# Zero-tile matmuls at the start, projection weights in quarters and a ring of six PSUM banks in a linear-attention and routed-FFN layer

## What is computed

```python
xn = _layernorm(x, axis=-1)
q = _phi((x @ W_Q.T).reshape(b, t, H, DK))      # attention: x is xn here
k = _phi((x @ W_K.T).reshape(b, t, H, DK))
v = (x @ W_V.T).reshape(b, t, H, DK)
S = g4 * S + jnp.einsum('bhi,bhj->bhij', kt, vt)     # scan over tokens
z = g3 * z + kt
num = jnp.einsum('bhij,bhi->bhj', S, qt)
den = jnp.sum(z * qt, axis=-1, keepdims=True) + EPS
y = (num/den * sigmoid(x @ W_g_w.T + W_g_b)) @ W_O.T
# FFN on xn: base = x @ W_lin.T + b_lin; top 2 of 8 experts, each left (D x 4), right (4 x D)
x = x + attention(xn) + ffn(xn)
```

## Time and profile before

| | us |
|---|---|
| median of 3 runs | 265.98 (265.62 to 266.72) |
| the profiled execution | 264.92 |
| its span, slowest core (core 3) | 263.9 |
| spans of the 8 cores | 262.6 to 263.9 |
| TensorE busy | 243.6 (92%) |
| VectorE / ScalarE / GpSimd busy | 162.8 / 79.5 / 61.7 |

### The profile page before, as it was taken

One profiled execution on the slowest core, in us unless ns is written; L12 is line 12 of the kernel. 1 busy time (PEld: TensorE's weight loads), 2 busy tenths in 40 slices (PEclk: granted clock), 3 DMA queues, 4 the chain that ended last, 5 costly groups with the idle time before them and its releaser, 6 DMA issues.

```text
span 263.9 us, 5412 instructions; the slowest of 8 cores (262.6 to 263.9 us)
## 1 busy us (share of the span) xinstructions
PE 243.6 (92%) x1768; PEld 122.6 (46%) x1768; DVE 162.8 (62%) x425; ACT 79.5 (30%) x132; POOL 61.7 (23%) x99
## 2 busy tenths in 40 slices
PE   0369999999889999999999999999999999999995
PEld 0233444454444555454545454445545555544442
DVE  5646374858766667565664657546556685686622
ACT  2644857375445222324333022111111201000000
POOL 2773000030505501314050403021304030333000
DMA  6999999999994022120404022122222123343223
GB/s 183 238 142 253 243 166 226 208 194 178 254 345 149 0 83 79 70 92 0 161 1 157 4 82 79 79 83 81 79 82 82 80 80 106 137 137 105 82 97 142
DMA packets 9615, 33.25 MB, mean 126 GB/s; under 512 B 1458, under 2 KB 1778, under 8 KB 9332
## 3 DMA queue, kind: packets, MB, share of 16 engines
q1 hardware_dynamic: 6692, 22.27, 24.8%
q0 software_dynamic: 2896, 10.64, 21.4%
HBM read 32.00 MB, written 8.39 MB: 153 GB/s over the span
## 4 chain that ended last, share of the span: by engine, by line
PE 84%; DVE 7%; issue 3%; DMA 3%; ACT 1%; SPq 0%; DVEq 0%; ACTq 0%
PE PJ L340 26%; PE L L362 17%; PE L L406 8%; PE PJ L333 7%; PE PJ L362 4%; PE L L340 4%; DMA x_sb<-x 3%; PE T L311 3%; PE L L333 2%; PE SY L354 2%; PE PJ L406 2%; PE T L347 2%; PE SY L378 1%; PE T L319 1%; PE T L392 1%
## 5 line engine op out<-in xcount | busy, mean ns | idle before, releaser
L362 PE MATMUL L<-wlin_sb,xnfm 128*128 128x512 bf16 x208 | 49.2, 379 | 0.0
L298 POOL TENSOR_SCALAR S_blk<-S_sb,small_s 128x260 bf16<-128x260 f32 x30 | 28.8, 973 | 85.8 <-DVE S_sb L775 85.6
L362 PEld LDWEIGHTS L<-wlin_sb,xnfm 128*128 128x128 bf16 x208 | 19.8, 98 | 23.2 <-issue 0.8
L844 ACT ACTIVATE e_sb<-PJ 128x512 bf16<-128x512 f32 x28 | 16.5, 593 | 42.1 <-PE PJ L340 40.6
L608 DVE TENSOR_SCALAR e_sb<-e_sb 128x512 bf16<-128x512 bf16 x32 | 9.4, 294 | 28.7 <-ACT e_sb L844 28.7
L820 ACT ACTIVATE xn_tm<-x_sb,nmr,rstd 128x1024 bf16<-128x1024 f32 x16 | 19.9, 1241 | 23.6 <-POOL nmr L254 22.1
L406 PE MATMUL L<-wo_sb,ygfm 128*128 128x512 bf16 x104 | 26.7, 379 | 0.0
L340 PE MATMUL PJ<-xnfm,wg_sb 128*128 128x512 bf16 x112 | 26.6, 379 | 0.0
L340 PE MATMUL PJ<-xnfm,wq_sb 128*128 128x512 bf16 x112 | 26.6, 380 | 0.0
L340 PE MATMUL PJ<-xnfm,wk_sb 128*128 128x512 bf16 x112 | 26.6, 380 | 0.0
L333 PE MATMUL PJ<-wv_sb,xnfm 128*128 128x512 bf16 x96 | 24.6, 400 | 0.0
(11 more groups left out here) (115 smaller groups left out, 357.0 us busy)
## 6 DMA issues: line engine op xcount, KB each, us to landing
ro_sb<-x SPq DMA_DIRECT2D x16, 512.0 KB, 4.0
out<-ro_sb SPq DMA_DIRECT2D x15, 512.0 KB, 2.7
x_sb<-x SPq DMA_DIRECT2D x10, 512.0 KB, 8.8
x_sb<-x POOLq DMA_DIRECT2D x6, 512.0 KB, 21.3
wlin_sb<-wlin POOLq DMA_DIRECT2D x1, 2048.0 KB, 38.9
wv_sb<-wv POOLq DMA_DIRECT2D x4, 256.0 KB, 10.9
wq_sb<-wq POOLq DMA_DIRECT2D x2, 512.0 KB, 18.2
wk_sb<-wk POOLq DMA_DIRECT2D x2, 512.0 KB, 24.7
```

The lines of the kernel that those rows point to most:

```text
L298: GP.tensor_scalar(S_blk[:, :].rearrange("p (q w) -> p q w", q=4)[:, :, 65 * e : 65 * e + 65], S_sb[:, :].rearrange("p (q w) -> p q w", q= ...
L362: TE.matmul(lb(c, n)[:, :], xnk(k, c), wlin_sb[:, D * k + 512 * n : D * k + 512 * n + 512], start=False, stop=False)
L844: SE.activation(e_sb[:, 512 * (n % 2) : 512 * (n % 2) + 512], bank[:, :], AF.Exp).then_inc(ac_e, 1)
```

## The change

Zero-tile matmuls (`warm`) run ahead of the first transpositions and at two later places; every projection weight comes in quarters, GpSimd's queue interleaves x4 to x7 with them and first waits for x1; SP's `small`, `cmat` and blin wait for the second quarter of wq. rstd of chunks 1 and 3 is made by GpSimd between its transfers. Six banks rotate. The programs of TensorE, VectorE and ScalarE for the opening are put in another order. The diff, cut to its core:

```diff
-    ring4 = [PJ[0], PJ[1], L[0], L[1]]
+    ring6 = [PJ[0], PJ[1], L[0], L[1], SYb[0], SYb[1]]
+    vb = [ring6[i] for i in (0, 1, 2, 3, 2, 1, 2, 1)]
+    qb = [ring6[i] for i in (4, 5, 0, 1)]
+    kb = [ring6[i] for i in (3, 4, 5, 0)]
+    gb = kb
...
         load_x(3)
+        SY.wait_ge(d_wq[1], 16)
         SY.dma_start(small[:, :], small_d[:, :]).then_inc(d_sm, 16)
...
-        SY.wait_ge(d_wg[1], 16)
+        SY.wait_ge(d_wg[3], 16)
...
+    def wload_q(dst, srcd, i, s):
+        o = 2 * FH * i
+        GP.dma_start(dst[:, o : o + 2 * FH], srcd[:, o : o + 2 * FH]).then_inc(s[i], 16)
...
     def rs(c):
+        j = {1: 0, 3: 1}.get(c, c - 6)
         GP.wait_ge(dv_st, c + 1)
...
-        GP.wait_ge(d_x[0], 16)
...
+        GP.wait_ge(d_x[1], 16)
+        wload_q(wv_sb, wv_d, 0, d_wv)
+        wload_q(wv_sb, wv_d, 1, d_wv)
+        rs(1)
+        wload_q(wv_sb, wv_d, 2, d_wv)
+        wload_q(wv_sb, wv_d, 3, d_wv)
+        wload_q(wq_sb, wq_d, 0, d_wq)
+        wload_q(wq_sb, wq_d, 1, d_wq)
+        rs(3)
         xload(4)
+        wload_q(wq_sb, wq_d, 2, d_wq)
+        wload_q(wq_sb, wq_d, 3, d_wq)
+        wload_q(wk_sb, wk_d, 0, d_wk)
+        wload_q(wk_sb, wk_d, 1, d_wk)
         xload(5)
-        wload_half(wq_sb, wq_d, 1, d_wq)
+        wload_q(wk_sb, wk_d, 2, d_wk)
+        wload_q(wk_sb, wk_d, 3, d_wk)
         xload(6)
+        wload_q(wg_sb, wg_d, 0, d_wg)
+        wload_q(wg_sb, wg_d, 1, d_wg)
         xload(7)
...
+    def warm(n):
+        for _ in range(n):
+            TE.matmul(SYb[1][:, :], S_blk[:, 0:128], S_blk[:, 0:512], start=True, stop=True)
...
     def pe_program():
+        TE.wait_ge(dv_z, 1)
+        warm(22)
         TE.wait_ge(d_id, 16)
         xtr(0)
+        warm(5)
         xtr(1)
...
+        TE.wait_ge(d_wv[0], 16)
+        vproj(0, vb[0], 0, 2)
+        warm(2)
+        TE.wait_ge(d_wv[1], 16)
+        vproj(0, vb[0], 2, 4)
...
+        TE.wait_ge(d_wv[3], 16)
+        for c in range(3):
+            vproj(c, vb[c], 6, 8)
+        TE.wait_ge(dv_xev, 4)
+        vproj(3, vb[3])
+        for i in range(4):
+            TE.wait_ge(d_wq[i], 16)
+            for m in range(4):
+                if i == 0 and m >= 2:
+                    TE.wait_ge(ac_v, m - 1)
+                fproj(wq_sb, 0, m, qb[m], pe_q, 2 * i, 2 * i + 2)
         xtr(4)
+        TE.wait_ge(ac_v, 4)
+        for i in range(4):
+            if i == 2:
+                TE.wait_ge(dv_xev, 5)
+                vproj(4, vb[4])
+            TE.wait_ge(d_wk[i], 16)
+            for m in range(4):
+                if i == 0 and m >= 1:
+                    TE.wait_ge(dv_q, m)
+                fproj(wk_sb, 0, m, kb[m], pe_k, 2 * i, 2 * i + 2)
+            if i == 2:
+                xtr(5)
         TE.wait_ge(dv_xev, 6)
+        TE.wait_ge(dv_q, 4)
+        vproj(5, vb[5])
+        for i in range(4):
+            TE.wait_ge(d_wg[i], 16)
+            for m in range(4):
+                if i == 0:
+                    TE.wait_ge(dv_k, m + 1)
+                fproj(wg_sb, 0, m, gb[m], pe_g, 2 * i, 2 * i + 2)
+            if i == 0:
+                xtr(6)
+            if i == 1:
+                TE.wait_ge(dv_xev, 7)
+                TE.wait_ge(ac_v, 5)
+                vproj(6, vb[6])
+            if i == 2:
+                xtr(7)
         TE.wait_ge(d_lg, 16)
         tgp(0)
-        for c in (6, 7):
-            TE.wait_ge(dv_xev, c + 1)
-            TE.wait_ge(ac_g, c - 5)
-            vproj(c, L[c - 6])
+        TE.wait_ge(dv_xev, 8)
+        TE.wait_ge(ac_v, 6)
+        vproj(7, vb[7])
...
     def dve_program():
+        VE.memset(S_blk[:, :], 0.0).then_inc(dv_z, 1)
...
         xev_v(3)
+        stats(4)
         VE.wait_ge(d_sm, 16)
...
+        phi(0, qb[0], fm(qfm, 0)[:, 0:512], dv_q)
+        phi(1, qb[1], fm(qfm, 0)[:, 512:1024], dv_q)
         VE.wait_ge(ac_dec, 2)
         VE.tensor_scalar(dk8a[:, :], nlg[:, 0:8], small[:, 16:17], None,
                          ALU.mult).then_inc(dv_dec, 1)
+        xev_v(4)
+        phi(2, qb[2], fm(qfm, 0)[:, 1024:1536], dv_q)
+        phi(3, qb[3], fm(qfm, 0)[:, 1536:2048], dv_q)
         VE.wait_ge(d_cm, 16)
...
         ins.then_inc(dv_mk, 1)
-        stats(4)
         stats(5)
...
         xev_v(5)
...
         stats(6)
+        for m in range(4):
+            phi(4 + m, kb[m], fm(kfm, 0)[:, 512 * m : 512 * m + 512], dv_k)
+        xev_v(6)
         stats(7)
-        VE.wait_ge(ac_mk, 1)
+        VE.wait_ge(ac_dec, 3)
         qt(0)
...
         for c in range(4):
             xn(c)
+        for c in range(4):
+            vev(c, vb[c])
+        SE.wait_ge(d_sm, 16)
+        SE.activation(nlg[:, :], small[:, 4:16], AF.Exp, scale=-1.0).then_inc(ac_dec, 1)
+        xn(4)
...
+        for m in range(2):
+            SE.wait_ge(pe_q, m + 1)
+            eexp(m, qb[m])
         SE.wait_ge(dv_dec, 2)
         SE.activation(dk8[:, :], dk8a[:, :], AF.Exp)
         SE.activation(gc4[:, :], nlg[:, 8:12], AF.Exp, scale=-128.0)
+        for m in range(2, 4):
+            SE.wait_ge(pe_q, m + 1)
+            eexp(m, qb[m])
         SE.wait_ge(d_cm, 16)
...
         SE.activation(masks[:, :], mtmp, AF.Exp).then_inc(ac_mk, 1)
...
         xn(5)
+        vev(4, vb[4])
         for m in range(4):
+            if m == 2:
+                xn(6)
+            SE.wait_ge(pe_k, m + 1)
+            eexp(4 + m, kb[m])
+        vev(5, vb[5])
         xn(7)
+        vev(6, vb[6])
         for m in range(4):
-            tanhg(0, m, ring4[(m + 2) % 4])
+            tanhg(0, m, gb[m])
         xn(8)
+        vev(7, vb[7])
         e8exp(0)
```

More of the change, by code:

```diff
@@ L131, in build_core @@
     d_lg = sem("d_lg")
-    d_wv, d_wq, d_wk, d_wg = ([sem(f"d_wv{i}") for i in range(4)], [sem("d_wqa"), sem("d_wqb")],
-                              [sem("d_wka"), sem("d_wkb")], [sem("d_wga"), sem("d_wgb")])
+    d_wv, d_wq = [sem(f"d_wv{i}") for i in range(4)], [sem(f"d_wq{i}") for i in range(4)]
+    d_wk, d_wg = [sem(f"d_wk{i}") for i in range(4)], [sem(f"d_wg{i}") for i in range(4)]
+    dv_z = sem("dv_z")
     d_wl, d_wo, d_rt = sem("d_wl"), sem("d_wo"), sem("d_rt")
@@ L412, in kproj @@
     def kproj(c):
-        TE.wait_ge(ac_g, c + 4)
+        if c == 0:
+            TE.wait_ge(ac_v, 8)
+        else:
+            TE.wait_ge(ac_g, c + 4)
         fproj(wk_sb, c // 4 + 1, c % 4, PJ[1], pe_k)
@@ L464, in pe_program @@
[L464 to L467, removed]
-        TE.wait_ge(dv_xev, 3)
-        xtr(4)
[L470 to L489, removed]
-        TE.wait_ge(dv_xev, 6)
[L491 to L499, removed]
+        TE.wait_ge(d_wv[0], 16)
[3 more added lines that the diff above has]
+        vproj(0, vb[0], 2, 4)
+        TE.wait_ge(dv_xev, 2)
+        vproj(1, vb[1], 0, 4)
+        xtr(2)
+        TE.wait_ge(d_wv[2], 16)
+        for c in range(2):
+            vproj(c, vb[c], 4, 6)
+        TE.wait_ge(dv_xev, 3)
@@ new lines, in pe_program @@
+        vproj(2, vb[2], 0, 2)
+        xtr(3)
+        vproj(2, vb[2], 2, 6)
+        TE.wait_ge(d_wv[3], 16)
[9 more added lines that the diff above has]
+                fproj(wq_sb, 0, m, qb[m], pe_q, 2 * i, 2 * i + 2)
+        xtr(4)
+        TE.wait_ge(ac_v, 4)
@@ L517, in pe_program @@
                 TE.wait_ge(dv_norm, c)
+            else:
+                TE.wait_ge(ac_g, 3)
             scores(c)
@@ L595, in stats @@
         VE.wait_ge(dv_st, c + 1)
-        if c < 8:
+        if c < 8 and c not in (1, 3):
             VE.tensor_scalar(nm[:, c : c + 1], mv[:, 2 * c : 2 * c + 1], -1.0, None,
@@ L704, in dve_program @@
         ins.then_inc(dv_mk, 1)
-        stats(4)
         stats(5)
-        xev_v(4)
-        for m in range(2):
-            phi(m, ring4[m], fm(qfm, 0)[:, 512 * m : 512 * m + 512], dv_q)
         xev_v(5)
-        for m in range(2, 4):
-            phi(m, ring4[m], fm(qfm, 0)[:, 512 * m : 512 * m + 512], dv_q)
         stats(6)
+        for m in range(4):
+            phi(4 + m, kb[m], fm(kfm, 0)[:, 512 * m : 512 * m + 512], dv_k)
+        xev_v(6)
         stats(7)
-        VE.wait_ge(ac_mk, 1)
+        VE.wait_ge(ac_dec, 3)
         qt(0)
-        for m in range(4):
-            phi(4 + m, ring4[(m + 2) % 4], fm(kfm, 0)[:, 512 * m : 512 * m + 512], dv_k)
-        xev_v(6)
         xev_v(7)
@@ L802, in xn @@
     def xn(c):
-        if c < 8:
+        if c < 8 and c not in (1, 3):
+            j = {0: 0, 2: 1}.get(c, c - 2)
             SE.wait_ge(dv_st, c + 1)
@@ L871, in act_program @@
             xn(c)
+        for c in range(4):
[3 more added lines that the diff above has]
+        xn(4)
         SE.wait_ge(dv_ini, 4)
-        SE.activation(nlg[:, :], small[:, 4:16], AF.Exp, scale=-1.0).then_inc(ac_dec, 1)
         SE.wait_ge(dv_dec, 1)
         SE.activation(nlg[:, :], nlg[:, :], AF.Ln, bias=one_c[:, :]).then_inc(ac_dec, 1)
+        for m in range(2):
+            SE.wait_ge(pe_q, m + 1)
+            eexp(m, qb[m])
         SE.wait_ge(dv_dec, 2)
```

58 lines of the change are left out of this document (13 added, 45 removed).

## The result

The changed kernel takes 277.92 us (median; 277.83 to 278.32), the kernel before, on the same chip, 265.92: a ratio of 1.0449, 95% interval 1.0424 to 1.0474. The forecast of 270.7 us had the direction; its range ended at 274.0. The profiled execution took 277.9 us, its slowest core (0) spans 276.7.

What follows compares the result with a forecast made beforehand. TensorE bounds the end, VectorE `tgp` to iteration 1. E 29.7, plus 29.2 to `tgp` and 15.6 to iteration 1, loses 4.75 us: 264.92 becomes 269.7, plus 1.06 to the median, 270.7 us; range 266.5 to 274.0.

Steps and rivals of the forecast that it cites:

- E: Start of the first exponential of q on ScalarE; forecast at 29.7 us, against 33.23 before.
- `small` at 22.3 + 0.1 + 4.0: On SP's queue, `small` waits for wq's second quarter (22.3), then takes 4.0 us like a residual row, landing at 26.4.
- a rival (0.07): On SP's queue `small` takes 8.6 us to land: +9.35 us, 275.3 us in all; chance 0.07.
- its sum 1.2 us lower: If DMA engines take queues in turn, `small` lands in about one turn and the sum is 1.2 us lower.
- The clock: TensorE's clock falls in waits of k's and g's first quarters; the one behind g costs 1.9 us: 272.6 us; chance 0.17.
- The chain from E to `tgp`: Evacuations make TensorE wait for banks and xn(5) in k and g: `tgp` starts at E + 29.2, against 20.9 before.
- Zero for the zero tiles: Opening: ten slow matmuls may speed up, worth 1.9 us of TensorE, but nothing on the path, since q awaits its weights.
- Zero for one v less behind `tgp`: Behind `tgp` `vproj(7)` stands alone where two did; costs nothing, since VectorE is the limit there.
- 27.5: Earliest E by DMA order: wq's last quarter lands at 26.9, then 2 matmuls; would give +2.6 us.
- 28.5: E if x4 decides: x4 lands at 23.9, then statistics 1.6, normalization 2.57 and Ln 0.4 us.
- v would end near 23.5 as before: If zero tiles do not raise the clock: v ends near 23.5, q's first block at 29.1, still before 29.7.
- break-even of 24.95: Value of E at which iteration 1, at E + 44.8, starts at 69.75 us as before.

Runs made afterwards that it cites:

- experiment 5: Changed kernel with `small` issued early and the decay tables and masks put back ahead of q on ScalarE and VectorE: 272.67 us, ratio 1.0234.
- experiments 3 and 4: 3: changed kernel without its 29 zero-tile matmuls, 278.52 us, ratio 1.0458. 4: kernel before with 22 and 5 zero-tile matmuls alone, 266.26 us, ratio 0.9992.
- experiment 1: Changed kernel without SP's wait for wq's second quarter, so small, cmat and blin are issued behind x3 again: 275.05 us, ratio 1.0336.
- experiment 11: Changed kernel, `small` early, tables ahead of q, phi of k first, v(6) behind `tgp`, x10 and x11 on GpSimd's queue ahead of wlin: 267.80 us, ratio 1.0075.

## Why the prediction was wrong in size

The steps of the prediction against core 0 of the changed kernel (a `*` marks core 2, where the clock held behind g's first quarter):

| step | forecast | measured |
|---|---|---|
| SP issues `small` | 22.4 us | 23.55 |
| `small` lands | 26.4 | 33.3 |
| E | 29.7 | 36.03 |
| k's first quarter ends | E + 5.6 | E + 5.56 |
| xtr(5) ends | E + 13.1 | E + 13.2 |
| g's first quarter ends | E + 21.4 | E + 21.8 (21.5*) |
| `tgp` starts | E + 29.2 | E + 30.8 (29.3*) |
| `tgp` to iteration 1 | 15.6 | 15.85 |
| iteration 1 to the third | 11.3 | 11.29 |

- **The step that failed** is the term "`small` at 22.3 + 0.1 + 4.0". wq's second quarter came 1.2 us later than its sum of bytes gave; then `small` took 9.7 us to land, 7.7 to 9.7 on the eight cores, where I had taken 4.0 from a residual row because that was alone in its queue. The same transfer's own row had 8.6 us. I had explained that number by the x ahead of it in the queue; behind nothing but a landed quarter it took as long. With ScalarE's part 0.6 us shorter than written, E was 36.03, 6.3 us late. The price belonged to a rival (0.07) and should have been the forecast.
- The Trainium skill (DMA: Bandwidth & Descriptors, section Queues, rings and completion order) has the engines take the queues in turn; by that the prediction made its sum 1.2 us lower. The changed kernel does not bear that out: on SP's queue `small` took 7.7 us at least.
- **The clock** was a rival of its own (0.17), and it came true beside the late `small`: from E to `tgp` core 0 took 1.55 us more than core 2. Its price, 1.9 us from the earlier trace rows, measured 1.68 in experiment 5. As the prediction said, the fall behind g's first quarter costs in full and one ahead of xtr(5) costs nothing, since xtr(5) waits for xn(5) anyway. The Trainium skill (TensorE: Matmul & The Clock Gate, Part 1) has the clock drop after idling, and the trace agrees: on core 0 it is 0.62 from 31 to 40 us, where TensorE idles for 5.45 us. Behind g's first quarter it fell with matmuls between waits of 0.30 to 1.34 us. The four cores where it held there (1, 2, 4 and 5) had the same waits, but their clock was still low in k's second quarter, where core 0 had 1.00 again; that made the wait of xtr(5) shorter (1.84 us on core 0). Core 2:

```profile
41.00:43.00 2.00, 2.00 (x6) 0.73 (x5) 2.00 (x6) 0.00 (x0) 1.88 (x4) 0.50 1.10 263
...
48.27 0.61 PE L327 MATMUL T<-ident_s,xn_tm 128*128 128x128 bf16 x8 [0.26 <-ACT xn_tm L858]
```

- **The chain from E to `tgp` held**, to 0.1 us where the clock held (29.26 to 29.27 on four cores). Zero for the zero tiles held as well (experiments 3 and 4), but not for the reason given, that q cannot finish before its weights: in the changed kernel `small` set E, and in experiment 1 v's end did. Zero for one v less behind `tgp` missed 0.25 us, because TensorE, which then waits longer for A_sb and slows down, was the limit in place of VectorE's list; with two v there (experiment 11) it is 15.57 to 15.60 us again.
- The sum closes: 6.3 us for E, 1.6 for the clock and 0.25 behind `tgp` are 8.2 us over the forecast's 269.7 for the profiled execution, so 277.9. The 1.06 us between the profile of before and its median had no counterpart after.
- **A second step failed behind the first**: q's wait for v was put at nothing. The bounds "27.5" (wq's last quarter) and "28.5" (x4) forgot that q starts when v is done, at 23.5 to 26.6 us, and needs 5.87 us to its first complete block: 29.4 to 32.4 (the text has 29.1, among the rivals only). That "v would end near 23.5 as before" was misread: before, q begins at 25.3 to 27.6 us on the eight cores, on core 3 with

```profile
27.58 1.89 PE L340 MATMUL PJ<-xnfm,wq_sb 128*128 128x512 bf16 x8
```

So even with `small` in time the slowest core could not have had E at 29.7; in experiment 1 it is 33.87. The break-even of 24.95 was out of reach with or without `small`. wg's last quarter landed at 50.9 us (issued at 22.8, and 28.1 to land), not by 45.8; g did not need it before 65.

The experiments split the loss, each step with the one before it:

| kernel | E, eight cores | E to `tgp`, clock held | us | ratio |
|---|---|---|---|---|
| changed | 33.85 to 36.57 | 29.27 | 277.92 | 1.0449 |
| `small` early (1) | 30.57 to 33.87 | 29.29 | 275.05 | 1.0336 |
| and tables ahead of q (5) | 29.22 to 33.14 | 26.66, worked out (28.34 as it fell) | 272.67 | 1.0234 |
| and phi of k first (9) | 30.14 to 33.87 | 25.11 | 269.69 | 1.0136 |
| and v(6) behind `tgp` (10) | 29.22 to 34.40 | 23.39 | 270.50 | 1.0157 |
| and x10 ahead of wlin (11) | 29.90 to 33.59 | 23.39 | 267.80 | 1.0075 |
| before | 31.83 to 33.23 | 20.93 | 265.92 | 1 |

Of 12.0 us, 10.1 come back by moving operations in the lists of five engines, with the six banks, the quarters and the zero tiles kept. What is left from E to `tgp` is the 2.47 us of waits for phi of four blocks and for one chunk. Why the cores spread by 4 us in E, with v's first matmul between 12.8 and 16.9 us, was not settled; on all eight cores of experiment 1 that matmul waited 1.4 to 3.2 us for wv.

## What to carry to other kernels

Before quarters or a longer ring of buffers are credited with anything, write down when each evacuation ends: if all blocks of a weight complete within one quarter, their evacuations come in a bunch, and every operation that stands among them on ScalarE or VectorE (masks, a normalization, statistics) can become a wait of TensorE, which here was often paid again through its clock (1.55 and 1.68 us). Keep small transfers that gate a whole engine ahead of the first large ones, and price a moved transfer by its own old row before any nearer-looking one.
